# Attention out-projection moved from float32 matmuls to float16 pieces

## The reference, cut to what matters

```python
def attn(x, Wq, bq, Wkv, bkv, Wo, bo):            # 16 query heads of 16, one shared key/value head
    q = (einsum('bte,oe->bto', x, Wq) + bq) * scaling
    k, v = split(einsum('bte,oe->bto', x, Wkv) + bkv)
    qr = q.reshape(bsz, NUM_HEADS * tgt_len, HEAD_DIM)
    attn_output = softmax(qr @ k.T) @ v
    attn_output = ...                              # back to (bsz, tgt_len, 256)
    return einsum('bte,oe->bto', attn_output, Wo) + bo      # the out-projection

xn = layernorm(x)
out = x + attn(xn, ...) + ffn(xn, ...)             # ffn: six low-rank experts, gated, with exp and log
```

## Time and profile before

| | us |
|---|---|
| median of 3 runs (lowest, highest) | 924.08 (920.78, 924.17) |
| the profiled execution's own time | 922.81 |
| its span, first to last instruction | 921.0 |
| PE busy | 857.4 (93%) |
| DVE busy | 780.7 (85%) |
| ACT busy | 673.2 (73%) |
| POOL busy | 512.8 (56%) |

### The profile page before, as it was taken

How to read it: one execution, slowest core, us unless ns; L and a number is a source line. 1 busy time by engine, 2 the same in 40 slices (tenths; PEclk the granted TensorE clock), 3 DMA queues, 4 the chain that set the end, 5 groups by cost and what they waited for, 6 DMA issues and landing times.

```text
span 921.0 us, 17722 instructions
## 1 busy us (share of the span) xinstructions
PE 857.4 (93%) x5845; PEld 282.1 (31%) x5845; DVE 780.7 (85%) x1490; ACT 673.2 (73%) x1369; POOL 512.8 (56%) x691
## 2 busy tenths in 40 slices
PE   4479999999999999999999999999999999999895
PEld 2223222332323333332323333332333333232222
DVE  6578898988989898998989898998989898899814
ACT  2115787787878778777877877787778778788880
POOL 2656566565666656565666647566666656534200
PEclk9676999999999999999999999999999999999998
DMA  3423243534524453543335353442444453331110
GB/s 96 97 66 60 74 92 92 117 83 116 113 75 105 107 114 94 124 87 108 95 94 111 94 116 87 129 100 86 96 113 104 104 115 84 92 94 61 48 60 34
DMA packets 125072, 86.04 MB, mean 93 GB/s; under 512 B 57143, under 2 KB 109112, under 8 KB 124984
## 3 DMA queue, kind: packets, MB, share of 16 engines
q1 hardware_dynamic: 124824, 84.82, 38.3%
q10 hardware_dynamic: 160, 0.10, 0.1%
HBM read 39.30 MB, written 33.54 MB: 79 GB/s over the span
## 4 chain that ended last, share of the span: by engine, by line
PE 78%; DVE 15%; issue 3%; POOL 2%; ACT 1%; DMA 1%; ACTq 0%; POOLq 0%; DVEq 0%
PE pO L364 24%; PE pA L346 18%; DVE M L808 9%; PE pB L351 8%; PE pA L481 5%; PE pA L428 5%; PE pA L499 4%; PE pA L483 3%; PE pA L417 3%; PE pA L453 2%; PE pA L468 2%; DVE st L728 2%; PE pB L461 1%; DVE RL L821 1%; PE pB L439 1%
## 5 line engine op out<-in xcount | busy, mean ns | idle before, releaser
L808 DVE TENSOR_REDUCE M<-pA 128x1 f32<-128x512 f32 x1024 | 652.3, 682 | 86.4 <-PE pA L346 82.3
L627 ACT ACTIVATE P<-pB 128x512 f32<-128x512 f32 x1002 | 552.6, 601 | 130.5 <-PE pB L351 126.0
L346 PE MATMUL pA<-K,Q 48*128 48x512 f16 x1024 | 326.0, 388 | 21.7 <-DVE M L808 11.8
L351 PE MATMUL pB<-Q,K 50*128 50x512 f16 x1002 | 317.8, 385 | 0.3 <-DVE M L808 0.3
L364 PE MATMUL pO<-P,VK 128*32 128x512 f32 x2048 | 273.7, 607 | 3.1 <-ACT OTr L633 2.0
L346 PEld LDWEIGHTS pA<-K,Q 48*128 48x128 f16 x1024 | 67.8, 94 | 343.6 <-DVE M L808 287.7
L954 POOL TENSOR_SCALAR Cz<-Cx 128x512 f32<-128x512 f32 x32 | 62.1, 1940 | 37.0 <-ACT Cx L609 37.0
L499 PE MATMUL pA<-wo,On 128*128 128x256 f32 x248 | 71.9, 414 | 2.7 <-DVE RL L821 2.7
L364 PEld LDWEIGHTS pO<-P,VK 128*32 128x32 f32 x2048 | 40.4, 108 | 99.3 <-issue 63.2
L351 PEld LDWEIGHTS pB<-Q,K 50*128 50x128 f16 x1002 | 64.3, 94 | 11.8 <-ACT P L627 10.3
L968 POOL TENSOR_TENSOR On<-Op,Rb 128x512 f32<-128x512 f32 x31 | 39.9, 1286 | 45.0 <-issue 41.2
(11 more groups left out here) (148 smaller groups left out, 806.6 us busy)
## 6 DMA issues: line engine op xcount, KB each, us to landing
o_parts<-OTr SPq DMA_DIRECT2D x62, 256.0 KB, 2.3
X<-in_x SPq DMA_DIRECT2D x16, 512.0 KB, 3.9
q_pieces<-Qp SPq DMA_DIRECT2D x64, 128.0 KB
out<-OUT SPq DMA_DIRECT2D x32, 256.0 KB, 3.9
Op<-o_parts SPq DMA_DIRECT2D x31, 256.0 KB
Rb<-l_parts SPq DMA_DIRECT2D x31, 256.0 KB
Q<-q_pieces SPq DMA_DIRECT2D x30, 256.0 KB, 4.8
Q<-q_pieces SPq DMA_DIRECT2D x34, 128.0 KB, 4.5
```

Of the source, the lines that this page charges most:

```text
L346: e.matmul(bank1("ab", t)[:, :], Q16[r:r + 48, b % 3, h, 128 * s:128 * s + 128], K16[r:r + 48, b % 3, :], start=True, stop=True).then_inc( ...
L351: e.matmul(bankB(t)[:, :], K16[r:r + 50, b % 3, 128 * i:128 * i + 128], Q16[r:r + 50, b % 3, :, 32 * hh:32 * hh + 32], start=True, stop=Tr ...
L627: e.activation(P[:, u % PR, :], bankB(u + LB)[:, :], ACT.Exp, scale=alpha).then_inc(S("e"))
L808: e.tensor_reduce(M[:, t // 32 % 2, t % 2, t % 32 // 2:t % 32 // 2 + 1], bank1("ab", t)[:, :], AX, ALU.max, negate=True).then_inc(S("mx"))
```

## The change

Each out-projection group becomes six float16 matmuls (three products of pieces for each half) in place of two float32 ones. For that:

- POOL, right behind each `on`, writes the high piece (a cast) and the low piece (a subtraction) of the divided values into `OnP`; PE now waits for the low piece.
- `Wo` gets high and low pieces `woP`, made at the start on ACT and DVE; its range joins the reduction of ranges. Its DMAs are issued from the ACT queue ahead of everything, where they stood in the SP queue behind the other weights.
- V is scaled by a power of two as it is copied out of PSUM (`vsc`), its bias beforehand; the factors cost some small instructions at the start. `fo` becomes a multiply by `scl[:, 9:10]` and an add in one instruction.
- `woL` (last half batch, still float32) is scaled once on POOL, ahead of the scaling of `W2`.

```diff
@@ ranges
+                    e.tensor_reduce(wmx[:, 3:4], wc[:, :, V0:V0 + D], XY, ALU.max,
+                                    apply_absolute_value=True).then_inc(S("wm"))
+                    w.wait_ge(S("vgb"), 64)
+                    e.tensor_reduce(bmx[:, 3:4], vgb[:, :], AX, ALU.max, apply_absolute_value=True).then_inc(S("wm"))
...
+                    w.wait_ge(S("wo"), 64)
+                    e.tensor_reduce(amx[:, 1:2], wo[:, :, :], XY, ALU.max,
+                                    apply_absolute_value=True).then_inc(S("wm"))
@@ TensorE
-                        w.wait_ge(S("on"), 2 * b + parts)
-                        w.wait_ge(S("wo"), 64)
+                        w.wait_ge(S("onl"), 2 * b + parts)
+                        w.wait_ge(S("wop"), 2)
                         for part in range(parts):
-                            mm = e.matmul(bank1(f"o{t}", b)[:, 0:C], On[:, b % 2, part, 128 * t:128 * t + 128],
-                                          wo[:, part, :], start=(part == 0), stop=(part == 1))
+                            for k, (wp, op) in enumerate(PIECES):
+                                mm = e.matmul(bank1(f"o{t}", b)[:, 0:C], OnP[:, b % 2, part, op, 128 * t:128 * t + 128],
+                                              woP[:, wp, part, :], start=(part == 0 and k == 0), stop=(part == 1 and k == 2))
@@ ScalarE
+            for k in range(4):
+                e.dma_start(wo[32 * k:32 * k + 32, :, :], ...).then_inc(S("wo"), 16)
...
                 if due("wdh", n) is not None:
+                    e.activation(woP[:, 0, :, :], wo[:, :, :], ACT.Identity, scale=scl[:, 3:4]).then_inc(S("wop"))
...
                     e.activation(VGs[:, :], bank2("vg", b)[:, 0:128], ACT.Identity,
-                                 scale=scl[:, 4:5], bias=vgb[:, 0:1]).then_inc(S("vge"))
+                                 scale=vsc[:, 0:1], bias=vgb[:, 0:1]).then_inc(S("vge"))
@@ VectorE
+                    e.scalar_tensor_tensor(out=woP[:, 1, :, :], in0=wo[:, :, :], scalar=scl[:, 3:4], in1=woP[:, 0, :, :],
+                                           op0=ALU.mult, op1=ALU.subtract).then_inc(S("wop"))
...
-                        e.tensor_tensor(OUT[:, t, :], bank1(f"o{t}", b)[:, 0:C], Rs[:, b % 5, t, :],
-                                        ALU.add).then_inc(S("fo"))
+                        e.scalar_tensor_tensor(out=OUT[:, t, :], in0=bank1(f"o{t}", b)[:, 0:C], scalar=scl[:, 9:10],
+                                               in1=Rs[:, b % 5, t, :], op0=ALU.mult, op1=ALU.add).then_inc(S("fo"))
@@ GpSimd
+                    w.wait_ge(S("woL"), 128)
+                    e.tensor_scalar(woL[:, :, :], woL[:, :, :], scl[:, 3:4], None, ALU.mult).then_inc(S("wos"))
                     e.tensor_scalar(W2[0:ER + 2, :], W2r[0:ER + 2, :], scl[0:ER + 2, 3:4], XS,
...
                     w.wait_ge(S("o"), 4 * (nh // 2 - 1))
-                    e.tensor_tensor(On[:, nh // 2 % 2, nh % 2, :].rearrange("p (t h) -> p h t", h=H),
-                                    Op[:, :].rearrange("p (h t) -> p h t", h=H),
+                    e.tensor_tensor(On[:, :].rearrange("p (t h) -> p h t", h=H), Op[:, :].rearrange("p (h t) -> p h t", h=H),
                                     Rb[:, :].rearrange("p (h t) -> p h t", h=H), ALU.mult).then_inc(S("on"))
+                    w.wait_ge(S("on"), nh + 1)
+                    e.tensor_copy(OnP[:, nh // 2 % 2, nh % 2, 0, :], On[:, :]).then_inc(S("onh"))
+                    w.wait_ge(S("onh"), nh + 1)
+                    e.tensor_tensor(OnP[:, nh // 2 % 2, nh % 2, 1, :], On[:, :], OnP[:, nh // 2 % 2, nh % 2, 0, :],
+                                    ALU.subtract).then_inc(S("onl"))
@@ SyncE
-            for k in range(4):
-                e.dma_start(wo[32 * k:32 * k + 32, :, :], ...).then_inc(S("wo"), 16)
```

More of the change, by code:

```diff
@@ L214, in build @@
         Op = sb("Op", [128, T])
-        On = sb("On", [128, 2, 2, T])
+        On = sb("On", [128, T])
+        OnP = sb("OnP", [128, 2, 2, 2, T], F16)
         OUT = sb("OUT", [128, 4, C])
@@ L226, in build @@
         wcP = sb("wcP", [128, 2, 2, WC], F16)
+        woP = sb("woP", [128, 2, 2, C], F16)
         BW = sb("BW", [128, 2, ER + 1])
@@ L242, in build @@
         prio = sb("prio", [128, NE])
[L243 to L248, removed]
+        wmx = sb("wmx", [128, 4])
+        amx = sb("amx", [128, 2])
+        bmx = sb("bmx", [128, 4])
+        rng = sb("rng", [128, 4])
+        two = sb("two", [1, 4])
+        fac = sb("fac", [1, 10])
         one = sb("one", [1, 128])
-        scl = sb("scl", [128, 8])
+        scl = sb("scl", [128, 10])
+        vsc = sb("vsc", [128, 1])
         R1 = [ps(f"pA{k}") for k in range(N1)]
@@ L276, in build @@
             "uk": lambda b: (S("uke"), b + 1), "q0": lambda b: (S("qe0"), b + 1), "q1": lambda b: (S("qe1"), b + 1),
-            "a": lambda b: (S("mm"), b + 1), "rg": lambda b: (S("two"), 1), "bs": lambda b: (S("scl"), 1),
+            "a": lambda b: (S("mm"), b + 1), "rg": lambda b: (S("two"), 2), "bs": lambda b: (S("scl"), 1),
             "o0": lambda b: (S("fo"), 4 * b + 1), "o1": lambda b: (S("fo"), 4 * b + 2),
@@ L371, in _ @@
                     w.wait_ge(S("rng"), 1)
-                    for k in range(3):
+                    for k in range(4):
                         mm = e.transpose(bank1("rg", 0)[0:1, 128 * k:128 * k + 128], rng[:, k:k + 1], idf[:, :])
@@ L388, in _ @@
                     w.wait_ge(S("ones"), 4)
-                    w.wait_ge(S("two"), 1)
-                    e.matmul(bank1("bs", 0)[:, 0:7], one[:, :], fac[:, 0:7], start=True, stop=True).then_inc(S("bs"))
+                    w.wait_ge(S("two"), 2)
+                    e.matmul(bank1("bs", 0)[:, 0:10], one[:, :], fac[:, 0:10], start=True, stop=True).then_inc(S("bs"))
                 for h in range(2):
@@ L514, in _ @@
                         if (b := due(f"{name}{t}", n)) is not None:
-                            w.wait_ge(S("woL"), 128)
+                            w.wait_ge(S("wos"), 1)
                             w.wait_ge(S("nl"), 4 * k + t + 1)
@@ L526, in _ @@
             alpha = e.alloc_register("alpha")
+            for k in range(4):
+                e.dma_start(wo[32 * k:32 * k + 32, :, :],
+                            woT.rearrange("(a c w r) n -> a w r c n", a=2, c=2, w=2)[k % 2, k // 2]).then_inc(S("wo"), 16)
             for n in ticks(*ACT_NAMES):
@@ L580, in _ @@
                     w.wait_ge(S("vg"), b + 1)
-                    w.wait_ge(S("vgb"), 64)
+                    w.wait_ge(S("vsc"), 6)
                     w.wait_ge(S("vt"), b)
                     e.activation(VGs[:, :], bank2("vg", b)[:, 0:128], ACT.Identity,
-                                 scale=scl[:, 4:5], bias=vgb[:, 0:1]).then_inc(S("vge"))
+                                 scale=vsc[:, 0:1], bias=vgb[:, 0:1]).then_inc(S("vge"))
                 if (b := due("vte", n)) is not None:
@@ L653, in _ @@
                     e.memset(bmx[:, 2:3], 0.0).then_inc(S("wm"))
+                    e.memset(bmx[:, 3:4], 0.0).then_inc(S("wm"))
                     w.wait_ge(S("wq"), 16)
@@ L665, in _ @@
                     e.tensor_reduce(bmx[:, 1:2], bk_s[:, :], AX, ALU.max, apply_absolute_value=True).then_inc(S("wm"))
+                    e.tensor_reduce(wmx[:, 3:4], wc[:, :, V0:V0 + D], XY, ALU.max,
+                                    apply_absolute_value=True).then_inc(S("wm"))
+                    w.wait_ge(S("vgb"), 64)
+                    e.tensor_reduce(bmx[:, 3:4], vgb[:, :], AX, ALU.max, apply_absolute_value=True).then_inc(S("wm"))
                     e.tensor_reduce(amx[:, 0:1], wc[:, :, :], XY, ALU.max,
                                     apply_absolute_value=True).then_inc(S("wm"))
-                    w.wait_ge(S("wm"), 6)
-                    e.tensor_tensor(wmx[:, 2:3], amx[:, :], wmx[:, 0:1], ALU.max).then_inc(S("wm"))
-                    w.wait_ge(S("wm"), 7)
+                    w.wait_ge(S("wo"), 64)
+                    e.tensor_reduce(amx[:, 1:2], wo[:, :, :], XY, ALU.max,
+                                    apply_absolute_value=True).then_inc(S("wm"))
+                    w.wait_ge(S("wm"), 10)
+                    e.scalar_tensor_tensor(out=wmx[:, 2:3], in0=amx[:, 0:1], scalar=amx[:, 1:2], in1=wmx[:, 0:1],
+                                           op0=ALU.max, op1=ALU.max).then_inc(S("wm"))
+                    w.wait_ge(S("wm"), 11)
                     e.scalar_tensor_tensor(out=rng[:, :], in0=wmx[:, :], scalar=float(C), in1=bmx[:, :],
@@ L678, in _ @@
                     w.wait_ge(S("ones"), 4)
-                    e.tensor_reduce(two[:, :], bank1("rg", 0)[0:1, 0:384].rearrange("p (k n) -> p k n", k=3), AX,
+                    e.tensor_reduce(two[:, :], bank1("rg", 0)[0:1, :].rearrange("p (k n) -> p k n", k=4), AX,
                                     ALU.max).then_inc(S("t0"))
@@ L688, in _ @@
                     e.reciprocal(fac[:, 3:4], two[:, 2:3]).then_inc(S("t0"))
```

(22 more changed lines are left out.)

## The result

The changed kernel took 941.59 us (median of 4 runs, 940.05 to 944.32) against 923.74: a ratio of 1.0203, 95% interval 1.0168 to 1.0238. The profiled execution took 940.05 us, its span is 938.2. It is slower by 1.7 to 2.4%; 935 had been predicted. The traced execution is the lowest of the four.

A forecast was written before the change was run, and what follows sets the result against it. PE was taken to set the pace, with DVE covering `o1` and `o2`. The terms -7.8 + 19.0 + 1.2 + 1.1 - 1.0 - 0.3 = +12.2 us on 922.8 gave 935; range for 8 in 10, 919 to 945.

The forecast's parts named there:

- the stall: PE waiting ahead of `pv` and `s` in each batch for exponentials held up behind `var`: 1.36 us, 14 times, +19.0 us.
- The matmuls: Out-projection groups take 0.76 us for 1.06; `o3` and `o0` each give 0.30 us, 26 groups, -7.8 us.
- the third rival: Stall as forecast, but matmuls give nothing because DVE is behind in `o3`'s and `o0`'s stretches too: 943 us, chance 0.12.
- `o1` and `o2` give nothing: Two out-projection groups in the stretch DVE covers: shorter matmuls gain nothing there; without that cover, 8.4 us more.
- The split, even half: Cast and subtraction on POOL behind even `on` delay `var` by 1.85 us; `s` comes 6.97 us behind `on`; +19.0 us.
- The odd half: Cast and subtraction on POOL behind odd `on` end before `o0` needs them: free, margin 1.2 us.
- The tail: Last four groups: twelve float16 matmuls at the low clock take 2.7 us for 3.68, -1.0; one group at 892.99, -0.3.
- The start: Added range and scaling work before the steady batches: +1.2 us, and scaling `woL` on POOL ahead of `xT`'s DMA, +1.1.
- The clock: Rival: PE's granted clock falls behind each stall, each batch losing some 1.5 to 3 us: 956 or more, chance 0.05.
- the stall does not bind: Rival: exponentials or `on` have more room than read, so PE never waits: 908 to 916 us, chance 0.12.
- half a stall: Rival: PE absorbs part of the stall, leaving 0.6 us per batch, so no change: 924 us, chance 0.12.

The follow-up runs named there:

- the last version: Changed kernel with even split at tick 46, later `woL` scaling, `pl` behind guard1 and statistics at ticks 18 to 29: 911.47 us (0.9886); repeated, 910.29 (0.9856).

## Why the prediction was right

The mechanism of the stall was right at each link. The sum is 5 us short in the span (12.2 against 17.2), mostly by one term, the gain of `o3`; the median lies another 1.5 us above the traced execution, and no trace shows that part. By the prediction's own steps:

- *The matmuls.* A group of 0.76 us: 516.89 to 517.65 above. Right. That `o3` and `o0` both give their 0.30 was the term that failed: `s` to `q1` fell by 0.29, not 0.60. I had looked for DVE as what could take it (the third rival) and found nothing there; it was ACT, held by POOL's guard a second time. With `pl` behind guard1 the stretch falls from 35.40 to 34.96; 0.14 of these 0.44 us the move gives the kernel before as well (35.69 to 35.55 in the usual batch), the other 0.30 is the missing group. 12 batches x 0.31 = 3.7 us of the miss.
- *`o1` and `o2` give nothing.* Right: with the split out of the way `q1` to `s` is 16.71 and 16.74, where it was 16.65. The excess over before has a candidate in `fo`, which takes 475 ns against 424 (nothing had been taken for it), twice in that stretch; this was not tested. That DVE held these groups is shown by the moved statistics, in part: in the usual batch the move takes 0.58 us from `q1` to `s` with float16 (16.76 to 16.18) and 0.23 with float32 (16.71 to 16.48).
- *The split, even half.* `var` starts 557.57 - 554.28 = 3.29 us behind `on` (3.23 forecast), `s` 7.04 (6.97). Mean stall against `q1`: 7.03 - 5.61 = 1.42 us (1.36). Their number was wrong: 13, not 14, for the last even `on` that I counted, 803.59, has no `var` behind it. 13 x 1.42 = 18.5 against 19.0: the two errors nearly cancel, which is luck.
- *The odd half* is free in the steady batches, as forecast: the kernel with the odd split alone has the period of the kernel before. The margin is not endless, as the one wait of 0.89 us in the last version shows.
- *The tail.* PE waited 0.98 us for the low piece ahead of the last `o0`, which had been taken for nothing. The granted clock was 0.50 there from 892.3 to 899.1, already ahead of that wait; the kernel before has 3.4 us of it at the same place, behind the same wait of 1.35 us for `M`. Whether the 0.98 us made it longer was not tested. PE in order of time, the clock in the stretches view below it:

```profile
891.12 0.22 PE L492 MATMUL pB<-idh,M 128*64 128x128 f16 x1 [1.35 <-POOL M L973]
...
894.88 1.46 PE L503 MATMUL pA<-woP,OnP 128*128 128x256 f16 x6 [0.98 <-POOL OnP L1003]
```
```profile
888.00:893.00 5.00, 3.21 (x23) 0.67 (x19) 1.99 (x4) 4.47 (x11) 2.06 (x5) 0.93 0.44 134
893.00:899.00 6.00, 5.02 (x24) 1.28 (x22) 0.48 (x1) 2.52 (x5) 1.74 (x2) 0.50 0.06 23
...
920.00:925.00 5.00, 3.82 (x27) 2.51 (x28) 1.81 (x4) 0.00 (x0) 0.00 (x0) 1.00 0.15 52
```

  The last twelve matmuls, forecast at 2.7 us at the low clock, took 1.48 us at a granted clock of 1.00, though PE had waited 2.35 us just before:

```profile
921.18 1.48 PE pA L503 x12
```

  They alone give 2.2 us where 1.0 was forecast. From the last `s` to the end the span is 0.6 us shorter than before (111.2 against 111.8), where 1.3 had been forecast: the term is half as large as forecast, and its parts went other ways than they were reckoned.
- *The start.* The DMA of the second batch's `xT` was issued at 46.59 where it had been 43.57: +3.0 us, 2.3 forecast. The ranges made 1.4 to 1.8 of it, `woL` 1.6: its instruction took 1.57 us, where twice L876's 0.554 had been taken for the same number of columns.
- *The clock* stayed at 1.00 through the steady batches of the traced execution, with 2.3 to 3.2 us of PE idle in each (0.9 before) and single waits of up to 1.41 us. So that rival fell here, but it is not excluded: in two kernels with the same stall, the later `woL` and the later `root`, the clock fell once, behind waits of 1.81 and 1.26 us, for 3.4 and 6.8 us. That makes two of the four traced executions with this stall, and none of the eight without it. What decides was not found, since a wait of 1.41 us left it at 1.00.

The account in the span: to the first `s` of the 13, +5.1 (start 3.0, the first stall 1.9, rest 0.2); 12 periods, 12 x 1.115 = +13.4; the interval behind the last stall -0.65; the tail -0.6; together 17.2. Against the forecast 3.7 us are the matmuls, 0.7 the start, 0.7 the tail, 0.2 the rest of the way to the first `s`, less 0.5 at the stall, which leaves 0.2.

The side rivals: *the stall does not bind* fell with the constant 7.03; *half a stall* likewise. Of the third, that the matmuls give nothing, half was true by another engine.

## What to carry to other kernels

Before work is put on an engine with room, read what stands behind it in that engine's queue and what its followers wait for: 1.85 us cost nothing at one tick and 1.4 us at another, in an engine that is idle 44% of the time. Where a distance between two steps wanders from batch to batch, its smallest value is the length of the path, and what lies above it is slack: here 5.61 - 5.16 = 0.45 us on average, which is why 1.85 us cost 1.4. Where it has become constant, the path sets the pace. A shorter instruction on the busiest engine gives only what the next engine lets through: here the place of the split took the ratio from 1.020 to 1.003, and three more moves in the order of other work (`woL`, `pl`, the statistics) to 0.986 and 0.989, of which two give 0.995 without the change.

## What the runs showed of the hardware

A GpSimd multiply of 128x512 by a per-partition scalar with one operation took 1.57 us, nearly three times the 0.554 us of a two-operation one of 128x256; a two-operation one of 128x512 with constants (L984) took 1.94 us. The VectorE multiply-add that reads PSUM took 475 ns for 128x256 where the plain addition took 424. The prediction had taken 1.1 us for the first and nothing for the difference of the second. The granted clock fell from 1.00 to 0.50 in the middle of steady batches behind single PE waits of 1.26 and 1.81 us, once each, and stayed at 1.00 behind waits of 1.41 us and, in the tail, of 2.35 us.
